# Step sizes of a state-space scan: four terms summed by identity products on TensorE, half a block per chunk, and eighteen input products a batch on GpSimd

## What is computed

```python
def _s6(x, A_log, D, x_proj_w, dt_proj_w, dt_proj_b):
    A = -jnp.exp(A_log)
    xp = jnp.einsum('bld,ed->ble', x, x_proj_w)
    d_rank = xp[..., :DT_RANK]
    Bm = xp[..., DT_RANK:DT_RANK + D_STATE]
    Cm = xp[..., DT_RANK + D_STATE:]
    delta = jax.nn.softplus(jnp.einsum('blr,dr->bld', d_rank, dt_proj_w) + dt_proj_b)
    deltaA = jnp.exp(jnp.einsum('bld,dn->bldn', delta, A))
    deltaB_u = jnp.einsum('bld,bln,bld->bldn', delta, Bm, x)
    def step(h, inp):
        dA_t, dBu_t, C_t = inp
        h = dA_t * h + dBu_t
        y = jnp.einsum('bdn,bn->bd', h, C_t)
        return (h, y)
    ...
    return y + x * D
...
x = x + _L0_attn_ref(_layernorm(x, axis=-1), ...)
x = x + _L0_ffn_ref(_layernorm(x, axis=-1), ...)
```

## Time and profile before

| | us |
|---|---|
| median of 3 runs | 4632.39 |
| lowest and highest | 4631.8, 4634.91 |
| the profiled execution | 4633.29 |
| its span in the profile | 4631.2 |

### The profile page before, as it was taken

The page is one execution under the profiler, slowest core; times in us unless marked ns, Lnnn a source line. Parts: engine busy times, 40 slices in busy tenths (PEclk is TensorE's granted clock), DMA queues, the critical chain, the costliest instruction groups (busy, mean ns, idle before and its releaser), DMA issues. The chain is left out here.

```text
span 4631.2 us, 57251 instructions
## 1 busy us (share of the span) xinstructions
PE 2756.0 (60%) x15526; PEld 1031.7 (22%) x15526; DVE 3891.5 (84%) x3306; ACT 2755.6 (59%) x4103; POOL 3544.4 (77%) x1796
## 2 busy tenths in 40 slices
PE   3555554546464646455554555454544289999997
PEld 1111121111111111111111111111111145555553
DVE  3999999999999999999999999999998644455552
ACT  5667777776767677776676677777664222222221
POOL 3999999999999999999999999999998100000000
PEclk7566565656565656565565656565655589999999
DMA  4354545363645455454545454636353300000000
GB/s 103 96 129 119 144 105 158 90 164 84 165 96 152 111 134 135 115 135 113 130 119 135 113 152 96 165 75 173 89 135 78 141 15 19 23 18 18 18 19 7
DMA packets 198208, 472.72 MB, mean 102 GB/s; under 512 B 60688, under 2 KB 61200, under 8 KB 197088
## 3 DMA queue, kind: packets, MB, share of 16 engines
q1 hardware_dynamic: 177136, 452.11, 38.3%
q0 software_dynamic: 20736, 16.88, 1.4%
HBM read 126.83 MB, written 73.43 MB: 43 GB/s over the span
## 5 line engine op out<-in xcount | busy, mean ns | idle before, releaser
L881 POOL TENSOR_TENSOR ch<-hid,cmat 128x1024 f32<-128x1024 f32 x1024 | 2389.2, 2358 | 56.0 <-DVE hid L735 38.2
L735 DVE TENSOR_TENSOR_SCAN hid<-decay,inp 128x1024 f32<-128x1024 f32 x1024 | 2290.7, 2273 | 36.1 <-ACT decay L602 28.3
L602 ACT ACTIVATE decay<-delr,a_neg 128x1024 f32<-128x1024 f32 x1024 | 1137.3, 1113 | 723.6 <-DVE hid L735 709.9
L399 PE MATMUL ps_y<-ch,nsum 128*32 128x256 f32 x8192 | 1006.1, 596 | 904.8 <-POOL ch L881 902.2
L724 DVE TENSOR_TENSOR inp<-dx,bmat 128x1024 f32<-128x1024 f32 x832 | 958.8, 1210 | 64.0 <-ACT dx L610 64.0
L399 PEld LDWEIGHTS ps_y<-ch,nsum 128*32 128x32 f32 x8192 | 259.5, 146 | 1617.4 <-POOL ch L881 1377.7
L408 PE MATMUL ps_y<-ident,ysb 128*128 128x128 f32 x512 | 169.1, 431 | 589.0 <-ACT ysb L617 575.9
L846 POOL TENSOR_TENSOR inp<-dxr,bmat 128x1024 f32<-128x1024 f32 x192 | 453.5, 2362 | 0.0
L394 PE MATMUL ps_y<-xhT,dskip 128*32 128x256 f32 x2048 | 270.1, 620 | 142.6 <-DVE xr L745 142.6
L1134 POOL DMA_INDIRECT out_rows<-row,idx_out x16 | 41.1, 2570 | 402.4 <-issue 221.3
L610 ACT ACTIVATE dx<-dxr 128x1024 f32<-128x1024 f32 x256 | 260.8, 1019 | 3.0 <-DMA dxr<-dxT 3.0
(11 more groups left out here) (165 smaller groups left out, 3842.4 us busy)
## 6 DMA issues: line engine op xcount, KB each, us to landing
dxr<-dxT SPq DMA_DIRECT2D x1024, 128.0 KB, 2.4
delr<-delT SPq DMA_DIRECT2D x1024, 128.0 KB, 2.4
xr<-in_x SPq DMA_DIRECT2D x32, 1024.0 KB, 6.4
bmat<-b_and_c SPq DMA_DIRECT2D x256, 128.0 KB, 3.3
cmat<-b_and_c SPq DMA_DIRECT2D x256, 128.0 KB, 2.9
x_rows<-xr SPq DMA_DIRECT2D x16, 2048.0 KB, 7.7
out_rows<-xr SPq DMA_DIRECT2D x32, 1024.0 KB, 4.3
w<-in_w SPq DMA_DIRECT2D x2, 4096.0 KB, 23.9
```

Of the source, the lines that this page charges most:

```text
L399: last = pe.matmul(ps_y[q * CH:(q + 1) * CH, 0:2 * P], nsum[:], ch[:, g, q * 2 * P:(q + 1) * 2 * P], start=False, stop=(g == GROUPS - 1))
L602: nc.scalar.activation(decay[:, g % 2, :], delr[:, c % 2, :], ACT.Exp, scale=a_neg[:, i:i + 1])\
L735: nc.vector.tensor_tensor_scan(hid[:, g, :], decay[:, g % 2, :], inp[:, g, :], 0.0, ALU.mult, ALU.add).then_inc(hid_ready, 1)
L881: nc.gpsimd.tensor_tensor(ch[:, g, :], hid[:, g, :], cmat[:, g, :], ALU.mult).then_inc(ch_ready, 1)
```

## The change

The four terms of a step size are no longer added by GpSimd. For each half block, ScalarE makes six functions of 512 columns in a row (`terms`), TensorE adds relu, t, 1+t's remainder and the logarithm by four products with the identity into the same bank `aux` (`add_terms`), and ScalarE copies the sum to `delT` (`copy_step`). GpSimd keeps one pass a block, the product with x (`delta_x`).

A half block takes a chunk and a bit: z in TensorE's place (c, 1), the functions in ScalarE's place 3 of c, the sum in TensorE's place (c, 3), the copy in ScalarE's place 1 of c+1. The chunks (`Z`) are 12 to 15 for blocks 0 and 1 of the next batch, and 0, 1, 4 and 5 for blocks 2 and 3 of this one. GpSimd's product follows (14, 2), (0, 2), (2, 2) and (6, 2).

GpSimd makes 18 input products a batch (`OWN`): group 3 of every chunk, and group 2 of chunks 3 and 4. VectorE makes 46 instead of 52. `SUMS1`, `SUMS2`, `MAKE_OUT`, `FINISH2` and `RW_COPY` are laid anew. Ahead of the loop, blocks 0 and 1 of batch 0 are made, half by half.

```diff
-SUMS1 = {(5, 2): range(0, 2), (5, 3): range(2, 5), (6, 0): range(5, 8), (6, 1): range(8, 11), (6, 2): range(11, 14), (6, 3): range(14, 17)}
-SUMS2 = {(0, 2): range(0, 3), (0, 3): range(3, 6), (1, 0): range(6, 8), (1, 1): range(8, 11), (1, 2): range(11, 13), (1, 3): range(13, 15), (2, 0): range(15, 17)}
-MAKE_OUT = ((3, 1), (3, 1), (3, 2), (3, 2), (3, 3), (3, 3), (3, 3), (3, 3))
+SUMS1 = {(5, 2): range(0, 3), (6, 0): range(3, 7), (6, 1): range(7, 9), (6, 2): range(9, 13), (6, 3): range(13, 17)}
+SUMS2 = {(0, 2): range(0, 3), (1, 1): range(3, 4), (1, 2): range(4, 6), (2, 0): range(6, 9), (2, 1): range(9, 12), (2, 2): range(12, 17)}
+MAKE_OUT = ((3, 2), (3, 2), (3, 3), (3, 3), (4, 0), (4, 0), (4, 1), (4, 1))
...
-RW_COPY = (2, 0)
+RW_COPY = (2, 2)
...
-FINISH2 = (2, 1)
+FINISH2 = (3, 0)
...
+            def add_terms(b, k, h):
+
+                aux_free(b, ("s", k, h))
+                pe.wait_ge(z_act, (b * KD * 2 + 2 * k + h) * ZACT + ZACT)
+                half = slice(h * HALF, (h + 1) * HALF)
+                pe.matmul(aux[:], ident[:], dxT[:, k, half], start=True, stop=False)
+                for term in (te[:, half], tu[:, half]):
+                    pe.matmul(aux[:], ident[:], term, start=False, stop=False)
+                pe.matmul(aux[:], ident[:], delT[:, k, half], start=False, stop=True).then_inc(aux_full, 1)
...
+                        if c in Z and g in (1, 3):
+                            ahead, k, h = Z[c]
+                            if not (ahead and final):
+                                (step_size if g == 1 else add_terms)(b + ahead, k, h)
...
                 nc.scalar.activation(te[:, half], aux[:], ACT.Abs, bias=dtb[:, k:k + 1]).then_inc(z_act, 1)
-                nc.scalar.activation(dxT[:, k, half], aux[:], ACT.Relu, bias=dtb[:, k:k + 1])\
+                act.wait_ge(z_act, n + 1)
+                nc.scalar.activation(te[:, half], te[:, half], ACT.Exp, scale=-1.0).then_inc(z_act, 1)
+                nc.scalar.activation(dxT[:, k, half], aux[:], ACT.Relu, bias=dtb[:, k:k + 1]).then_inc(z_act, 1)
+                act.wait_ge(z_act, n + 2)
+                nc.scalar.activation(tu[:, half], te[:, half], ACT.Identity, bias=1.0).then_inc(z_act, 1)
+                nc.scalar.activation(delT[:, k, half], te[:, half], ACT.Ln, bias=1.0).then_inc(z_act, 1)
+                act.wait_ge(z_act, n + 4)
+                nc.scalar.activation(tu[:, half], tu[:, half], ACT.Identity, scale=-1.0, bias=1.0)\
                     .then_inc(aux_emptied, 1)
...
+            def copy_step(b, k, h):
+                aux_filled(b, ("s", k, h))
+                nc.scalar.activation(delT[:, k, h * HALF:(h + 1) * HALF], aux[:], ACT.Copy).then_inc(aux_emptied, 1)
...
+            def delta_x(b, par, k):
+
+                pool.wait_ge(aux_emptied, b * NUSE + USE[("s", k, 1)] + 1)
+                i, j = xhat_slot(k, par)
+                nc.gpsimd.tensor_tensor(dxT[:, k, :], delT[:, k, :], xhT[:, i, j, :], ALU.mult)\
+                    .then_inc(dx_made[k], 1)
```

More of the change, by code:

```diff
@@ L415, in _ @@
                 project(0, 0, h)
-            for k in range(3):
+            for k in range(2):
                 for h in range(2):
                     step_size(0, k, h)
+                    add_terms(0, k, h)
             pe.wait_ge(dskip_ready, KD)
@@ L494, in copy_proj, with terms @@
                                      ACT.Copy).then_inc(aux_emptied, 1)
[L496 to L507 removed]
+            def terms(b, k, h):
+                if has(b, 1) and h == 0:
+                    for s in dx_rep + del_rep:
+                        act.wait_ge(s, (b * (CHUNKS // 2) - CHUNKS // 2 + 2 * k + 2) * 16 * NT)
@@ L636, in _ @@
                 copy_proj(0, h)
-            for k in range(3):
-                if k == 2:
+            for k in range(2):
+                if k == 1:
                     copy_dx(0, 0)
```

147 lines of the change are left out of this document (52 added, 95 removed), and 3 rows, old and new, of the table DELTA.

## The result

| | us |
|---|---|
| median of 4 runs, before | 4633.48 |
| median of 4 runs, after | 4828.35 (4821.22 to 4833.9) |
| ratio, 95% interval | 1.0417, 1.0402 to 1.0433 |
| forecast | 4675, range 4572 to 4790 |

The change costs 195 us. The forecast had the sign and most of the mechanism, but the time lies 38 us above its range.

A forecast was written before the change was run, and what follows sets the result against it. VectorE (212.1 us a batch) and GpSimd (about 216) were taken as level bounds. A batch goes from 219.0 to 221.05: +30 over fifteen, -3 for the last, +16 for the first, so +43 on 4632.39: 4675 us, range 4572 to 4790.

The forecast's parts named there:

- VectorE's work, 205.3 us: VectorE's own work a batch: 212.1 us less six products of 1.13 us each that go to GpSimd.
- rival 4: GpSimd is not relieved and VectorE's 6.9 us of waits a batch stay: +110 on the forecast, 4785 us; chance 0.03.
- The chain from T0: From the end of a chunk's last scan: functions, TensorE's sum, turn; y at T0+11.15, wanted by VectorE at 9.99.
- rival 2: TensorE's clock is high when each sum starts: sum 3.5 us, no stall, 4541 us; chance 0.28.
- copy_rw's 5.9 us: ScalarE, chunk 2: the router copy moves to place 2 behind five squares; VectorE's router sums stall 5.9 us a batch.
- Chunks 6 and 7: ScalarE's moved queues: in chunk 6 a stall of 1.2 us; in chunk 7 a decay about 0.6 us late.
- Stall 1.15 us in each chunk behind one of the eight.: VectorE waits 1.15 us for y in the chunks behind those with a sum: 13, 14, 15, 0, 1, 2, 5, 6.
- start after the decay at T0+0.04, so at T0+1.1: ScalarE's six functions start 1.1 us after the end of a chunk's last scan, behind a decay.
- 6.2 to the next issue: TensorE's four-term sum takes 6.2 us until the next issue, from a burst starting at the low clock.
- 2.3 us late for two chunks: GpSimd: an extra pass behind chunks 14, 0, 2 and 6 makes it 2.3 us late for two chunks.
- The first batch: Half blocks made ahead of the loop delay its start, 22.4 us at decay (0, 2); net +16 us.
- The third rival: TensorE stays at the low clock in Z's chunks, 14.7 us a chunk against 12.5, stalls 2.2: 4805 us; chance 0.12.

The follow-up runs named there:

- f1_three: Changed kernel with copy_rw in place (2, 1), no loop on any engine, and z half a chunk earlier in chunks 12 and 4: 4661.92 us, ratio 1.0051.
- e1_rw: Changed kernel with the copy of the router's weights in place (2, 1) instead of (2, 2): 4722.56 us, ratio 1.0192.
- e7_z_early: Changed kernel with TensorE making z behind group 0's state sum instead of group 1's in chunks 12 and 4: 4788.78 us, ratio 1.0338.
- e6_before_dx_late: Kernel before, with only GpSimd's product for dx of the next batch's block 0 moved from (13, 3) to (14, 2): 4747.61 us, ratio 1.0246.
- e5_no_spread: Changed kernel with B and C spread over the partitions for batch 0 alone, later batches reusing them: 4744.99 us, ratio 1.0241.
- e3_unrolled: Changed kernel with the sixteen batches written out, no loop on any engine: 4800.17 us, ratio 1.0356.
- f2_turn: f1_three, and in addition SyncE issues two groups of the next batch's B ahead of its first dx: 4643.78 us, ratio 1.0021.

## Why the prediction missed

**What held.** VectorE's work, 205.3 us. The old waits gone with GpSimd's twelve passes (rival 4 is out). The chain from T0 in chunks 13 and 14: functions to T0+4.55, sum 6.2 us, y at T0+11.15 (11.3 in the row above). The clock low at the start of 108 of 114 sums, which puts rival 2 out for this kernel; f1_three reached its 3.8 us in one chunk of the eight. copy_rw's 5.9 us, measured 5.94, where e1_rw shows that it is a wait by itself. Chunks 6 and 7. Chunk 2's stall came out 0.36 below the forecast by two errors: its functions start 0.4 us later than T0+1.1, and its sum takes 5.2 us and not 6.2.

**What failed.**

1. *"Stall 1.15 us in each chunk behind one of the eight."* The term was taken from one position and multiplied by eight. In chunks 12 and 4 z is made late: the functions start at T0+2.24 and T0+2.00, not T0+1.1, their sums take 6.5 and 6.4 us, not 6.2, and the stalls behind are 2.86 and 2.49. Missed: 3.05 us a batch. The step that failed is "start after the decay at T0+0.04, so at T0+1.1": it asked when ScalarE is free, and not whether its input is there. A row of before at the low clock (two records of z in 2.07 us) was there to price it with. A second step is "6.2 to the next issue" as one price for all: e7_z_early took back 2.7 us a batch (40/15), and most of that by sums of 4.6 and 4.0 us.
2. *The turn of the batch, not priced.* The prediction counts the passes behind chunks 14, 0, 2 and 6 only as time of GpSimd's ("2.3 us late for two chunks"). It does not ask what the product moved from (13, 3) to (14, 2) holds up in SyncE's queue, and so puts that at nothing without a reason. The queue's only long pause there was 2.9 us, and the product is 5.4 us later (15.5 - 10.2). The 16 DMA engines had no room either (share 1.05), and GpSimd's step-size product of 2.3 us stands behind the late C. e6_before_dx_late gives that one entry a price of 114 us on the old kernel, where it comes 9.2 us later; e5_no_spread gives the turn 83 us on the new one, 5.3 a batch in the trace (230.6 - 225.3), against 6.1 missed in chunks 0 and 1.
3. *The loop's jump, not priced.* Once VectorE has nothing queued behind the jump, 28 us (e3_unrolled); a part of point 2's 83, since both edits remove it.
4. *The first batch:* +22 for +16.

Points 1 and 2 are (3.05 + 6.1) x 15 = 137 us, point 4 another 6, of 153. Some 6 us more are stalls 0.1 to 0.35 us longer than forecast, less chunk 2's; the last few are spread between the runs' medians.

The third rival gave 4805, near the time, by another way: stalls of 2.2 everywhere from a TensorE at the low clock throughout. It did not happen: four of the eight stalls lie at 1.55 or less, and the clock in chunks 12 to 15 was 0.75.

**Where the change's gain went.** It removes 13.7 us a batch (6.9 of waits, 6.8 of products) and adds 25.3: for y about 14, the router 5.9, the rest decays, the jump and B. With the router's copy, z, the jump and a part of the turn mended and all four terms summed (f2_turn), it stands at 1.0021 of the kernel before. A batch then takes 218.5 us, where the kernel before takes 219.0 and 218.4 unrolled: the sums and the full turn eat the gain just up. What is left over is the first batch, which still ends 19 us later (318.84 against 299.77).

## What to carry to other kernels

When a step is moved, walk the queue that takes up its result: in order, each entry behind the moved one is late by as much as that queue has no pause. Count the issue time, and ask whether the DMA engines have room for the transfers when they come in one row. A stall worked out for one place holds for the others only after each one's inputs have been timed there. And before work is moved from a full engine to one that is on the chain of waits, ask whether it has to be done: leaving out two terms that cancel but for rounding, and giving GpSimd three more products in their place brought 2.9%; moving four terms cost 4.2%.
